# A convolution, scan and attention hybrid on one core: B rows put into PSUM by TensorE, and ScalarE's pointer operands folded into matrix products

## The reference, cut to what matters

```python
# x: (8, 96, 64, 64). Layer 0, on group-normed x as (batch, 4096, 96):
xz = u @ in_proj_w.T; xm, z = xz[..., :192], xz[..., 192:]
xm = silu(conv4(xm) + conv_b)              # 4 taps along the sequence, per channel
dbl = xm @ x_proj_w.T                      # dt (6), B (16 states), C (16 states)
delta = softplus(dt @ dt_proj_w.T + dt_proj_b)
h[t] = exp(delta[t] * A) * h[t-1] + delta[t] * B[t] * xm[t]    # 192 channels x 16 states
y = sum_over_states(h[t] * C[t]) + xm * D
y = (y * silu(z)) @ out_proj_w.T           # then layer norm, gamma, beta, + x
# Layer 1: token norm (x-m)/sqrt(v+1e-5), linear attention (6 heads, no softmax), + residual,
# token norm, FFN 96 -> 384 -> 96 with e5m2 rounding of operands, + residual
```

## Time and profile before

| what | before |
|---|---|
| device time, 3 runs | 2514.06 us median (2513.1 to 2515.68) |
| profiled execution | span 2508.8 us; no time beside the span is given for it, the runs' median is 5.3 us above it |
| DVE busy | 2454.5 us, 98% |
| POOL busy | 2414.8 us, 96% |
| ACT busy | 2314.7 us, 92% |
| PE busy | 2142.1 us, 85% (matmuls overlap, so this is not its peak) |
| mean granted TensorE clock | 0.987 |

### The profile page before, as it was taken

How to read it: one execution, slowest core, us unless ns; L and a number is a source line. 1 busy time by engine, 2 the same in 40 slices (tenths; PEclk the granted TensorE clock), 3 DMA queues, 4 the chain that set the end, 5 groups by cost and what they waited for, 6 DMA issues and landing times.

```text
span 2508.8 us, 35019 instructions
## 1 busy us (share of the span) xinstructions
PE 2142.1 (85%) x10314; PEld 826.0 (33%) x10314; DVE 2454.5 (98%) x2391; ACT 2314.7 (92%) x3960; POOL 2414.8 (96%) x655
## 2 busy tenths in 40 slices
PE   6788888888888888888888888888888888888878
PEld 3334434323323323323333323323323333333323
DVE  7999999999999999999999999999999999999986
ACT  5777777999999999999999999999999999999977
POOL 4999999999999999999999999999999999999991
PEclk8999999999999999999999999999999999999979
DMA  6555555556656656566566566566566565566542
GB/s 243 189 185 172 195 185 184 202 198 207 209 202 205 207 201 212 201 205 206 204 206 214 194 208 212 195 210 208 198 210 211 197 207 201 192 206 203 186 142 75
DMA packets 171388, 494.54 MB, mean 197 GB/s; under 512 B 23072, under 2 KB 44704, under 8 KB 154240
## 3 DMA queue, kind: packets, MB, share of 16 engines
q1 hardware_dynamic: 171200, 492.30, 57.9%
HBM read 400.33 MB, written 91.88 MB: 196 GB/s over the span
## 4 chain that ended last, share of the span: by engine, by line
POOL 40%; issue 40%; DVE 15%; PE 3%; ACT 1%; DMA 0%; POOLq 0%; DVEq 0%; SPq 0%; ACTq 0%
POOL R L676 20%; DVE R L1277 11%; POOL D L649 9%; POOL R L672 7%; POOL du L642 3%; DVE D L1261 2%; POOL D L658 2%; PE G L1568 1%; PE Y L1568 0%; DVE q L1357 0%; DVE dl L1287 0%; DVE G L1302 0%; DVE h L1471 0%; DVE h L1478 0%; PE Y L1645 0%
## 5 line engine op out<-in xcount | busy, mean ns | idle before, releaser
L1277 DVE TENSOR_TENSOR_SCAN R<-DA,R,D 128x512 f32<-128x512 f32 x1344 | 1630.2, 1263 | 1.0 <-ACT DA L840 1.0
L840 ACT ACTIVATE DA<-ds,kept_w 128x512 f32<-128x512 f32 x1536 | 1054.8, 688 | 139.9 <-DVE R L1277 127.1
L676 POOL TENSOR_TENSOR R<-R,Cs 128x2048 f32<-128x2048 f32 x255 | 970.9, 3819 | 4.0 <-DVE R L1277 2.6
L649 POOL TENSOR_TENSOR D<-us,Bs 128x2048 f32<-128x2048 f32 x193 | 736.9, 3818 | 8.8 <-DMA us<-lo_d 8.8
L672 POOL TENSOR_TENSOR R<-R,Cs 128x4096 f32<-128x4096 f32 x64 | 476.5, 7446 | 0.1
L1261 DVE TENSOR_TENSOR D<-us,PB 128x2048 f32<-128x2048 f32 x191 | 356.8, 1868 | 6.3 <-DMA us<-lo_d 6.3
L1645 PE MATMUL Y<-R,kept_w 128*32 128x512 f32 x2048 | 266.1, 615 | 13.9 <-POOL R L672 12.8
L1602 PE MATMUL G<-un,wcv 96*128 96x512 f32 x512 | 251.6, 614 | 29.5 <-ACT h L907 29.5
L1277 DVE TENSOR_TENSOR_SCAN R<-DA,D 128x512 f32<-128x512 f32 x192 | 221.7, 1204 | 2.1 <-ACT DA L840 2.1
L1605 PE MATMUL G<-un,wcv 96*64 96x256 f32 x1024 | 138.5, 392 | 60.1 <-ACT xq L888 58.9
L1568 PE MATMUL G<-st,kept_w 128*64 128x256 f32 (+1 forms) x384 | 108.9, 485 | 53.5 <-ACT st L802 53.5
(11 more groups left out here) (240 smaller groups left out, 3437.5 us busy)
## 6 DMA issues: line engine op xcount, KB each, us to landing
Bs<-bc_d SPq DMA_DIRECT2D x128, 512.0 KB, 5.6
us<-lo_d SPq DMA_DIRECT2D x64, 1024.0 KB, 6.3
ds<-lo_d SPq DMA_DIRECT2D x64, 1024.0 KB, 8.4
Cs<-bc_d SPq DMA_DIRECT2D x128, 512.0 KB, 4.7
us<-hi_d SPq DMA_DIRECT2D x64, 512.0 KB, 6.8
ds<-hi_d SPq DMA_DIRECT2D x64, 512.0 KB, 5.5
lo_d<-dl SPq DMA_DIRECT2D x64, 256.0 KB, 2.0
lo_d<-du SPq DMA_DIRECT2D x64, 256.0 KB, 2.0
```

The source lines that it names most:

```text
L649: nc.gpsimd.tensor_tensor(shaped(D[:, s % NDBU, :, :], s), low(us, s) if s in LOWS else high(us), of_states(Bs, s), ALU.mult).then_inc(don ...
L676: nc.gpsimd.tensor_tensor(shaped(R[:, s, :, 0:T], s), shaped(R[:, s, :, 1:S], s), of_states(Cs, s), ALU.mult).then_inc(hc_done.sem, 1)
L840: nc.scalar.activation(DA[j % NDA][:, :], ds[:, i, :], ACT.Exp, scale=A[:, j:j + 1]).then_inc(exp_done.sem, 1)
L1277: nc.vector.tensor_tensor_scan(R[:, s, q, 1:S], DA[j % NDA][:, :], D[:, s % NDBU, q, :], before, ALU.mult, ALU.add).then_inc(scanned.sem, 1)
```

## The change

`put_b` moves from ACT to PE. It becomes a product of a 0/1 matrix `bsel` (32 rows, 128 columns, one for each of the three quads) with the B rows of st, straight from st and no longer from Bs; the result lands in PB. For this, st holds B and C in rows 0 to 31 and becomes a double buffer (ACT writes rows 0 to 63 by a plain copy; row 64 is a constant 1). PE's places for it: `put_b(g, 1)` as the first of the iteration; `put_b(g, 3)` after `out_proj(g-1)`; `put_b(g+1, 0)` after `variance(g-1, 1)`. ACT loses three biases read through a pointer: conv_b becomes row 96 of the convolution's tap 0, against a row of ones in un; dt's bias sits in row 64; 1e-5 becomes row 96 of `avg`, against rows of ones in sq and fsq. DVE sets these four rows once at the start.

```diff
@@ buffers and semaphores
-        wcv = sb("wcv", [C, TAPS, 2 * LOW])
+        wcv = sb("wcv", [C + 1, TAPS, 2 * LOW])
-        un = sb("un", [C, HALO + T])
+        un = sb("un", [C + 1, HALO + T])
-        st = sb("st", [128, T])
+        st = sb("st", [128, 2, T])
-        sq = sb("sq", [C, T])
+        sq = sb("sq", [C + 1, T])
-        fsq = sb("fsq", [C, T])
+        fsq = sb("fsq", [C + 1, T])
@@ SP, start
+            sp_eng.dma_start(wcv[C:C + 1, 0, :], I["conv_b"]).then_inc(cb_in, 16)
@@ ACT
-                    nc.scalar.activation(u[:, place(k) % 2, part(v)], src[v], ACT.Silu, bias=cb[:, v:v + 1])\
+                    nc.scalar.activation(u[:, place(k) % 2, part(v)], src[v], ACT.Silu)\
             def state_rows(k, src):
                 act.wait_ge(back_mm.sem, back_mm.at(k, 1))
-                act.wait_ge(back_mm.sem, back_mm.at(k - 1))
-                if there(k - 1):
-                    act.wait_ge(bc_out, count(k - 1, 16, 16))
-                nc.scalar.activation(st[:, :], src[:, :], ACT.Identity, bias=one_row).then_inc(st_done.sem, 1)
+                act.wait_ge(b_put.sem, b_put.at(k - 2))
+                if there(k - 2):
+                    act.wait_ge(bc_out, count(k - 2, 16, 16))
+                nc.scalar.copy(st[0:64, k % 2, :], src[0:64, :]).then_inc(st_done.sem, 1)
-            def put_b(k, s):
-                if k == 0 and s == 1:
-                    return
-                h, w = LOWS[s]
-                if s == 3 and place(k + 3) == 0 and later(k + 3):
-                    act.wait_ge(gn_act.sem, gn_act.at(k + 3, 4))
-                act.wait_ge(b_in[h], count(k, 16, 16))
-                act.wait_ge(dbu_d.sem, dbu_d.at(k, BY_DVE[s] - steps_to(k, s)))
-                n = SPLIT.get(s, T)
-                nc.scalar.copy(PB[:, 0:n], Bs[:, h, w, 0:n]).then_inc(b_put.sem, steps_to(k, s))
-                nc.scalar.activation(rs[:, :], src[0:C, :], ACT.Ln, bias=epsn[0:C, :]).then_inc(post_ln.sem, 1)
+                nc.scalar.activation(rs[:, :], src[0:C, :], ACT.Ln).then_inc(post_ln.sem, 1)
-                nc.scalar.activation(frs[:, :], src[0:C, :], ACT.Ln, bias=epsn[0:C, :]).then_inc(f_ln.sem, 1)
+                nc.scalar.activation(frs[:, :], src[0:C, :], ACT.Ln).then_inc(f_ln.sem, 1)
@@ ACT, iteration: the three calls of put_b are gone
@@ DVE, start
             step(nc.vector.memset(bsa[:, :, :], 1.0 * GT))
+            step(nc.vector.memset(sq[C:C + 1, :], 1.0))
+            step(nc.vector.memset(fsq[C:C + 1, :], 1.0))
+            step(nc.vector.memset(un[C:C + 1, :], 1.0))
+            step(nc.vector.memset(st[64:65, :, :], 1.0))
@@ PE
+            pe.wait_ge(cb_in, 16)
-                    last = one(o[:, :], dtw[:, 0:LOW], st[:, :])
+                    last = one(o[:, :], dtw[0:65, 0:LOW], st[0:65, k % 2, :])
+            def put_b(k, s):
+                if k == 0 and s == 1:
+                    return
+                if s == 3 and place(k + 3) == 0 and later(k + 3):
+                    pe.wait_ge(gn_act.sem, gn_act.at(k + 3, 4))
+                pe.wait_ge(st_done.sem, st_done.at(k))
+                pe.wait_ge(dbu_d.sem, dbu_d.at(k, BY_DVE[s] - steps_to(k, s)))
+                n = SPLIT.get(s, T)
+                one(PB[:, 0:n], bsel[:, BY_DVE[s] - 1, :], st[0:2 * STATE, k % 2, 0:n]).then_inc(b_put.sem, steps_to(k, s))
@@ PE, iteration
                 if g == 0:
                     pe.wait_ge(w_ready, 1)
+                if there(g):
+                    put_b(g, 1)
                 if there(g - 1):
                     add_skip(g - 1, 1)
...
                     out_proj(g - 1, G1)
+                if there(g):
+                    put_b(g, 3)
...
                     variance(g - 1, 1, G2)
+                if there(g + 1):
+                    put_b(g + 1, 0)
```

More of the change, by code:

```diff
@@ L777, in norm @@
                     act.wait_ge(front_mm.sem, front_mm.at(k - 1))
-                    nc.scalar.copy(un[:, 0:HALO], zero[0:C, 0:HALO])
-                nc.scalar.activation(un[:, lo:], un[:, lo:], ACT.Identity, bias=cgs[:, 1:2],
+                    nc.scalar.copy(un[0:C, 0:HALO], zero[0:C, 0:HALO])
+                nc.scalar.activation(un[0:C, lo:], un[0:C, lo:], ACT.Identity, bias=cgs[:, 1:2],
                                      scale=cgs[:, 0:1]).then_inc(normed.sem, 1)
@@ L862, in last_square @@
                     act.wait_ge(half_mm[h], 2)
-                nc.scalar.activation(sq[:, HALVES[h]], src[0:C, HALVES[h]], ACT.Square)\
+                nc.scalar.activation(sq[0:C, HALVES[h]], src[0:C, HALVES[h]], ACT.Square)\
                     .then_inc(half_act[h], 1)
@@ L871, in last_ln @@
                     act.wait_ge(post_dve.sem, post_dve.at(LAST - 1, 2))
-                nc.scalar.activation(rs[:, HALVES[h]], src[0:C, HALVES[h]], ACT.Ln, bias=epsn[0:C, :])\
+                nc.scalar.activation(rs[:, HALVES[h]], src[0:C, HALVES[h]], ACT.Ln)\
                     .then_inc(half_ln[h], 1)
@@ L936, in iteration @@
                 if there(g):
-                    put_b(g, 1)
                     decay(g, 0, 1)
@@ L974, in iteration @@
                     decay(g, 2, 1)
-                    put_b(g, 3)
                 if there(g + 1):
@@ L1031, in iteration @@
                     decay(g, 5, 0)
-                if there(g + 1):
-                    put_b(g + 1, 0)
                 if g == LAST:
@@ L1087, in beginning @@
             def beginning():
-                nc.scalar.copy(un[:, 0:HALO], zero[0:C, 0:HALO])
+                nc.scalar.copy(un[0:C, 0:HALO], zero[0:C, 0:HALO])
                 act.wait_ge(x_in, 16)
                 act.wait_ge(gn_act.sem, gn_act.at(0))
-                nc.scalar.activation(un[:, HALO:], un[:, HALO:], ACT.Identity, bias=gsh[:, :],
+                nc.scalar.activation(un[0:C, HALO:], un[0:C, HALO:], ACT.Identity, bias=gsh[:, :],
                                      scale=gsc[:, :]).then_inc(normed.sem, 1)
@@ L1096, in beginning @@
                     act.wait_ge(front_mm.sem, front_mm.at(0, 1 + v))
-                    last = nc.scalar.activation(u[:, 0, part(v)], src[:, 0:T - H * v], ACT.Silu, bias=cb[:, v:v + 1])
+                    last = nc.scalar.activation(u[:, 0, part(v)], src[:, 0:T - H * v], ACT.Silu)
                     last.then_inc(silued.sem, 1)
@@ L1116, in beginning @@
                 act.wait_ge(w_ready, 1)
-                put_b(0, 0)
                 act.wait_ge(silued.sem, silued.at(1))
@@ L1601, in conv @@
                     if v == 0:
-                        last = mm(o[:, :], wcv[:, t, 0:LOW], un[:, t:t + T], start=(t == 0), stop=(t == TAPS - 1))
+                        last = mm(o[:, :], wcv[0:rows_of(t), t, 0:LOW], un[0:rows_of(t), t:t + T], start=(t == 0), stop=(t == TAPS - 1))
                         continue
                     for rows, cs in halves():
-                        last = mm(o[rows, 0:H], wcv[:, t, LOW:LOW + HIGH], un[:, t + cs.start:t + cs.stop],
+                        last = mm(o[rows, 0:H], wcv[0:rows_of(t), t, LOW:LOW + HIGH],
+                                  un[0:rows_of(t), t + cs.start:t + cs.stop],
                                   start=(t == 0), stop=(t == TAPS - 1))
@@ L1611, in z_proj @@
                 if v == 0:
-                    last = one(o[:, :], wz[:, 0:LOW], un[:, HALO:])
+                    last = one(o[:, :], wz[:, 0:LOW], un[0:C, HALO:])
                 else:
                     for rows, cs in halves():
-                        last = one(o[rows, to:to + H], wz[:, LOW:LOW + HIGH], un[:, HALO + cs.start:HALO + cs.stop])
+                        last = one(o[rows, to:to + H], wz[:, LOW:LOW + HIGH], un[0:C, HALO + cs.start:HALO + cs.stop])
                 last.then_inc(front_mm.sem, 1)
@@ L1630, in dt_proj @@
                 if v == 0:
-                    last = one(o[:, :], dtw[:, 0:LOW], st[:, :])
+                    last = one(o[:, :], dtw[0:65, 0:LOW], st[0:65, k % 2, :])
                 else:
                     for rows, cs in halves():
-                        last = one(o[rows, 0:H], dtw[:, LOW:LOW + HIGH], st[:, cs])
+                        last = one(o[rows, 0:H], dtw[0:65, LOW:LOW + HIGH], st[0:65, k % 2, cs])
                 last.then_inc(back_mm.sem, 1)
@@ L2008, in beginning @@
                 z_proj(1, 0, DA[0])
+                pe.wait_ge(w_ready, 1)
+                put_b(0, 0)
             beginning()
@@ L2150 @@
         "skip": skip,
-        "one_row": (row == RANK)[:, None], "mask": (c[:, None] // hd == c[None, :] // hd) * hd ** -0.5,
+        "mask": (c[:, None] // hd == c[None, :] // hd) * hd ** -0.5,
     }
```

41 lines of the change are left out of this document (23 added, 18 removed).

## The result

The changed kernel takes 2517.27 us (median of 20 runs, 2512.99 to 2524.62); the kernel before, beside it, 2512.76 us (20 runs, 2509.01 to 2515.86). The ratio is 1.002, 95% interval 1.0012 to 1.0028: some 4.5 us more, under the 5.0 us that the prediction took as telling, but clear of no change by its interval. In a second series it was 2519.08 against 2511.3 us, ratio 1.0029 [1.002, 1.0039], some 7.5 us. The forecast was +3.0 us with a range of 2512.5 to 2523.5; the time lies in it, the difference is larger than forecast, and the point fits so well only because the kernel before stood 1.3 us lower in these runs than in the three shown ahead.

The account below looks back on a forecast made before the run. DVE and POOL, full and feeding each other, were taken to bound the kernel. 2.05 - 0.15 (shorter ACT work at the start) + 1.0 + 0.5 - 0.4 = +3.0 us on 2514.06 gave 2517.1 us; bounds 2514.7 to 2519.6, 8-in-10 range 2512.5 to 2523.5.

Parts of the forecast that it names:

- Steady chunks at 0: Three places of put_b on PE: PE's idle time and small slack hide the added 2.3 us a chunk, costing 0.
- (1) The start, 2.05 us: Four memsets ahead of the statistics: 2.80 us less 0.75 of DVE's idle time, 2.05 us delay; bounds 1.9 and 2.8.
- (2) The second chunk, +1.0: New product between z_proj and add_skip at low clock delays DVE's inputs and POOL: +1.0 us, bounds 0.9 and 1.9.
- (3) The last chunk, +0.5: Last chunk: DVE waits for ACT's exponential, which waits for the variance behind put_b(g, 3): +0.5 us, bounds 0 and 1.0.
- (4) the tail, -0.4: After the last scan: four or five shorter logarithms on the path, 0.09 us each: -0.4 us, bounds 0 and -1.0.
- ACT's freed time at 0: Steady part: ACT freed of some 2.0 us a chunk, worth 0 on the path since DVE is full.
- the rival of 0.03: ACT was the bound in small pieces, below what idle times show: 3 us in all, 2514 us; chance 0.03.
- The pointer's 0.09 us: ACT's silus and logarithms: each operation losing its bias pointer gets 0.09 us shorter, 0.5 us a chunk at most.
- PE gates every chunk: Rival: PE's places lack slack, so DVE waits 0.1 to 0.3 us a chunk: 2523 to 2536 us; chance 0.17.
- its point of decision: PE gating every chunk sets in from about 0.1 us more per product than the 0.95 us taken.
- POOL gets faster as ACT's reads fall: Rival: less SBUF contention speeds POOL's product, 2.7 us: 2514.4 us, or 2512 if DVE gained too; chance 0.10.
- The start hides the memsets: Rival: transfers or the clock set the start and second chunk, hiding memsets and product: 2514.0 us; chance 0.07.

Follow-up runs that it names:

- The fifth experiment: Changed kernel with its memsets moved behind the first statistics, and each product into PB issued twice: 2607.46 us, ratio 1.038 to the kernel before.
- the fourth experiment: Changed kernel with fourteen filler products instead of eight ahead of the first group product on TensorE: 2512.26 us, ratio 1.0006 to the kernel before.
- the second experiment: Kernel before, with only four memsets of the same sizes on a spare buffer ahead of the first statistics: 2515.5 us, ratio 1.0019.
- the first, without memsets ahead: Changed kernel with its four memsets moved behind the first statistics, where nobody waits: 2512.81 us, ratio 0.9998 to the kernel before.
- The seventh run: Changed kernel with memsets behind the statistics, and quad 1's row of the second chunk copied by ScalarE: 2512.17 us, ratio 1.0001 to the kernel before.
- the eighth's: Changed kernel, memsets behind the statistics, quad 3's product ahead of the dt projections, second chunk's quad 1 copied by ScalarE: 2509.22 us, ratio 0.9985.
- the ninth's: Kernel before, with TensorE held once in each of four chunks ahead of the x projection: 2531.87 us.
- The third experiment: Changed kernel with the B copies back on ScalarE, folded biases, double buffer st and memsets kept: 2513.41 us, ratio 1.0011 to the kernel before.
- the eleventh run: The changed kernel unaltered, run and profiled once more: 2519.08 us, ratio 1.0029 to the kernel before.

## Why the prediction was right, and where it was not

**The sum.** +3.0 was forecast, the medians moved by 4.5 and 7.8 us and the spans by 5.0 and 6.3. It came this near because errors of both signs met: the start was 5.8 and 4.9 us dearer than forecast, the chunks 3 to 62 1.8 us cheaper, and the last chunk and the tail together 1.8 us cheaper in one profile and 0.4 dearer in the other. That is luck and not the working.

**Steady chunks at 0: right.** 32 rows cost 1.05 us (taken 0.95, bounds 0.86 and 1.13), 232 columns 0.58 (taken 0.43), and the places held: from 400 to 2390 us DVE waited 0.9 us for PE's sums and 0.9 us for ACT's exponential, in eleven places. The fifth experiment bears out that little was left at DVE's second gate: of 1.05 us more of PE's work there, 0.97 came back as a wait. Its 1.5 us a chunk are for all three products doubled, so they do not price this one place.

**(1) The start, 2.05 us: wrong, the main error.** The step that failed is "DVE was idle 0.90 us there for the data": the idle time stands unchanged behind the memsets, so they count in full. And each was taken as 0.56 us, from a row whose next memset had no wait, where it costs 0.65: 3.14 us in all, beyond the upper bound of 2.8. Three costs were missing. TensorE's filler was cut to end where the statistics used to be ready; 3.14 us later it left 2.82 us of idle time, and the ten passes after it ran at the lower level: 2.6 us, shown by the fourth experiment. The transfer ahead of POOL's first D took 1.5 and 0.5 us more; that part varies from run to run and was not isolated. And DVE's first scan lost 0.4 to 0.5 us behind ACT's first decay. Together 6.8 to 7.7 us at chunk 0; the second experiment gives 4.06 of it with memsets alone, and the first, without memsets ahead, leaves 1.01.

**(2) The second chunk, +1.0: right in mechanism, and in size by the clock.** The product costs there 1.1 to 1.2 us at the lower clock, as before had it, and 0.6 at the full one, under the lower bound of 0.9. The two profiles' 0.8 are only alike by chance: the first has it in the second chunk, the second has -0.1 there and 0.9 in the chunk after, for a reason not traced. The seventh run takes the product out and the chunk falls to 37.43.

**(3) The last chunk, +0.5, and (4) the tail, -0.4.** -0.1 and +0.5, then -1.6 and 0.0: over the runs (the fifth apart) the last chunk took 36.0 to 39.3 us. The longest, 38.4 and 39.3, had a granted clock of 0.68 and 0.63 from 2410 to 2420 us, against 0.83 in before, but the eighth's 37.3 had 0.66, so the clock alone does not settle it. One kernel without products into PB, the ninth's, took 37.5, so these products are not needed for it. The logarithms' 0.4 cannot be seen in this.

**ACT's freed time at 0: wrong by 1.8 us.** "Its worth on the path is 0 in the steady part" was read from stretches; it does not hold in the chunks ahead of a new batch, where ScalarE has the group norm's squares as well. In chunk 22 of before DVE waits for ACT's exponential, and POOL then for DVE:

```profile
882.24 0.76 DVE L1302 SCALAR_TENSOR_TENSOR G<-G,kept_w,rs 96x512 f32<-96x512 f32 x1 [0.24 <-ACT rs L855]
...
908.41 3.81 POOL L676 TENSOR_TENSOR R<-R,Cs 128x2048 f32<-128x2048 f32 x1 [0.35 <-DVE R L1277]
```

After, the same two rows have no wait, and the chunk takes 37.50 instead of 37.86 us:

```profile
890.28 0.74 DVE L1291 SCALAR_TENSOR_TENSOR G<-G,kept_w,rs 96x512 f32<-96x512 f32 x1
...
916.43 3.81 POOL L677 TENSOR_TENSOR R<-R,Cs 128x2048 f32<-128x2048 f32 x1
```

Five such chunks, and one in which the gain is 0.15, make 1.9 us. The third experiment shows that ACT's relief is the cause. It is the rival of 0.03 in a place of its own: ACT was the bound in small pieces, worth 1.9 us and not the 3 that the rival named.

ACT's relief itself was smaller than the 128 us forecast: its busy time fell by 88.4 us and not to 2187 (2226.3), and its waits for DVE reached 198.4 and not 250 us. The pointer's 0.09 us holds (the silu now takes 598 ns, the norms' logarithm 583 instead of 675). The summed durations fell by some 130 us, but neighbouring instructions overlap in the trace by about 0.1 us, so a copy that goes frees less than its duration; an estimate from that is 19 us for the 191 copies, and the rest was not traced.

**The rivals.** "PE gates every chunk" did not come true. The product came out at its point of decision, 0.1 us above what was taken, and the steady chunks still did not grow; with another 1.05 us at each place they did. "POOL gets faster as ACT's reads fall" falls: the one-quad product took 3833 ns from 400 to 1200 us:

```profile
L677 POOL TENSOR_TENSOR R<-R,Cs 128x2048 f32<-128x2048 f32 x85 | 324.5, 3833 | 0.5
```

By the Trainium skill, page "SBUF — State Buffer", section "Who interferes with whom", the shift from ACT to PE should leave POOL's time alone. The trace agrees that nothing fell; the 11 ns more, 0.3%, have no cause shown. "The start hides the memsets" was the opposite of what happened.

**What stays open.** Why the changed kernel's medians lie 1.7 and 2.1 us above its profiled executions, and its longest runs 6.7 and 9.1 us. The long runs have the lower granted clock, by the figures under the eleventh run, but which chunks lose it and why was not seen. One chunk at the lower level cost 7 us in one execution with products into PB, and 1.05 us in one without; the falls differed in length (17 and 11 us), so that the product into PB makes them dearer is argued, not shown.

## What to carry to other kernels

Work placed ahead of the first instruction of the chain that everything waits for counts in full, and once more if TensorE was kept busy up to a fixed time: stretch the filler with it, or place the work behind. An idle time before an instruction is cover only when what ends it moves independently of what you add; ask which instructions stand in between. An average over a long stretch hides the few chunks that carry extra work: read one chunk of each kind before pricing an engine's freed time at nothing.
